# Projecting q and k transposed in the first stage of an AdaLN attention and mixture-of-experts block

## The chip, the cores and the metric

The kernel runs on one core of a Trainium2 chip. A core has five engines with a queue of their own each: TensorE (PE; PEld is its weight load), VectorE (DVE), ScalarE (ACT), GpSimd (POOL) and SyncE (SP), which here only issues DMAs. They work side by side and wait for each other through semaphores. SBUF is the working memory of 128 partitions, PSUM the memory of eight banks (128 x 512 float32 each) that TensorE writes. The metric is the time on the device in microseconds (us); lower is better.

## The reference, cut to what matters

```python
# x: (16, 1024, 256) float32; 16 heads of 16 numbers
mod = (silu(c) @ wmod).reshape(16, 6, 1, -1)      # sa, ca, ga, sb, cb, gb
h = layernorm(x) * (1 + ca) + sa
# attention of h:
xn = (h - mean(h)) * rsqrt(var(h) + 1e-5) * ln_gamma + ln_beta
q, k, v = heads(xn @ Wq + bq), heads(xn @ Wk + bk), heads(xn @ Wv + bv)
# rotation: x1 = even, x2 = odd numbers of a head
rot = stack([x1 * cos - x2 * sin, x1 * sin + x2 * cos], -1)
probs = softmax(causal(rot(q) @ rot(k).T / 4))
x = x + ga * (h + (probs @ v) @ Wo + bo)
h = layernorm(x) * (1 + cb) + sb
x = x + gb * moe_ffn(h)      # 8 experts, 512 chosen rows each, gathered and scattered
```

The change concerns everything from `h` up to the rotated q and k, and the constants that it needs.

## The kernel before, in words

The program is five stages, one after the other, with a barrier of all engines between two of them. `phase0` loads weights and makes the modulation rows and the biases. `phase1` normalises twice, projects q, k and v, rotates q and k and stores them. `phase2` is the attention, `phase3` the output projection and the residual, `phase4` the experts.

`phase1` goes over 16 batches of 1024 rows, eight tiles of 128 rows (T = 8) each. The order on every engine is written out by hand. The function `both(fr, bk)` does the "back" of one batch (`bk`: transpose, project, rotate, store) tile by tile, with pieces of the "front" of the next (`fr`: the two normalisations) put between the tiles. Buffers that hold a batch are double (index `p`), those of a tile too (`t % 2`).

Per tile of the back: PE transposes the normalised rows `xn` (L675), ACT copies them to `x_t` (L552), and PE projects: a bias row by a matmul with three rows of ones (L686) and two matmuls (L688) for q and k together, 128 x 512, then the same for v, 128 x 256. The weights move through the array and the rows of `x_t` are stationary, so rows lie on partitions in the result. DVE multiplies the 512 columns by cosines (L474) and by sines (L475), and adds the two results crosswise with strides (L481, twice 256 columns). PE transposes the rotated tile (L696), and only now do the numbers of a head lie on partitions. The result is kept as three bfloat16 parts: ACT casts the high part (L569), DVE takes the rest (L490), ACT casts the middle part (L575), POOL takes the low part (L641). ACT copies v to `v_st` (L561).

Per batch of the front: DVE takes the statistics of x (L419, L427) and inverts the deviation (L434, L436), ACT makes `h1`, the normalised x (L545), POOL multiplies and adds the modulation (L625, L627) and forms the residual in two more passes (L634, L636). DVE takes the statistics of h (L443, L450), ACT the root (L537), and DVE writes `xn` by eight tensor_scalar instructions in a row after tile 6 (L456, L461). SP loads the batch three ahead, stores the residual (L371), v (L377), and then q and k in 24 DMAs of 64 partitions (L383).

A PSUM bank serves one purpose: 0 and 1 the transposed rows, 2 and 3 q and k of a tile, 4 and 5 v, 6 and 7 the transposed q and k.

Of the kernel before, what the change touches and what calls it, by code (L numbers as in the profile page):

```python
# [25 lines left out]
P = 128  # L26
HEADS = 16
NG = 4
# [32 lines left out]
def build(nc, a, out):  # L61
# [14 lines left out]
    bias_d = nc.dram_tensor("bias_parts", [3, 3 * D], BF16, kind="Internal").ap()  # L76
# [11 lines left out]
    with ExitStack() as outer:  # L88
# [3 lines left out]
        rope = keep("rope", [P, T, 2 * DH], F32)  # L92
        w_all = keep("w_all", [P, KC, 3 * D], F32)
        wo = keep("wo", [P, KC, D], F32)
        bias3 = keep("bias3", [3, 3 * D], BF16)
# [3 lines left out]
        phase0(nc, a, ps, ident, mask, rope, w_all, wo, bias3, ones3, mods_d, bias_d, out_bias_d, b2_d, tok_d)  # L99
        phase1(nc, x, ps, ident, rope, w_all, bias3, ones3, mods_d, resid_d, q_d, k_d, v_d)  # L100
# [6 lines left out]
def phase0(nc, a, ps, ident, mask, rope, w_all, wo, bias3, ones3, mods_d, bias_d, out_bias_d, b2_d, tok_d):  # L107
# [3 lines left out]
    T = rope.shape[1]  # L111
    scale = (D // HEADS) ** -0.5
    with ExitStack() as ctx:
# [10 lines left out]
        brow = sb("brow", [1, 3 * D], F32)  # L124
# [8 lines left out]
        beff = sb("beff", [1, 3 * D], F32)  # L133
        beff_rest = sb("beff_rest", [1, 3 * D], F32)
        beff3 = sb("beff3", [1, 3, 3 * D], BF16)
# [11 lines left out]
        bias_done = sem("p0_bias_done")  # L147
        rows_done = sem("p0_rows_done")
# [11 lines left out]
            (brow[:, 0:D], a["L0_attn_bq"].rearrange("(o n) -> o n", o=1)),  # L160
            (brow[:, D:2 * D], a["L0_attn_bk"].rearrange("(o n) -> o n", o=1)),
            (brow[:, 2 * D:3 * D], a["L0_attn_bv"].rearrange("(o n) -> o n", o=1)),
# [9 lines left out]
        ]  # L172
        LOADED = DMA * (len(loads) + len(small))

        @block.sync
        def _(sp):
            for dst, src in loads:
                sp.dma_start(dst, src).then_inc(loaded, DMA)
            with nc.allow_non_contiguous_dma("one column per contraction chunk"):
# [17 lines left out]
        def _(act):  # L197
            act.wait_ge(loaded, LOADED)
            nc.scalar.activation(e[:, :], c[:, :], ACT.Exp, scale=-1.0).then_inc(exp_done, 1)

        @block.tensor
        def _(pe):
# [12 lines left out]
            for bank, lo, hi in ((4, 0, 2 * D), (5, 2 * D, 3 * D)):  # L215
                for k in range(KC):
                    last = pe.matmul(ps[0:1, bank, 0:hi - lo], beta[:, k:k + 1], w_raw[:, k, lo:hi],
                                     start=(k == 0), stop=(k == KC - 1))
# [1390 lines left out]
```

## Time and profile before

| | |
|---|---|
| median of 3 runs | 3257.47 us (3256.44 to 3257.87) |
| profiled execution | 3256.85 us, its span 3255.1 us |
| busy, whole span | PE 91%, DVE 72%, ACT 53%, POOL 31% |
| mean granted TensorE clock | 0.952 of 2.4 GHz |
| phase0 | 0 to 47 us |
| phase1 | 47 to 763 us |
| phases 2 to 4 | 763 to 3255 us |

The span is what the profiler saw between the first and the last instruction; 1.75 us lie around it. A busy time counts an instruction from its start to its end, whatever it waits for in between; neighbouring instructions of one engine overlap by some tenths of a microsecond, so the distance from one start to the next says what an instruction costs in a queue, and the duration what its result costs to wait for. The granted clock is 1.00 (2.4 GHz) or 0.50 (1.2 GHz) at any instant, and between them only as a mean.

### The profile page before, as it was taken

What the parts mean: (1) busy time and instruction counts of PE and PEld (TensorE: products, weight loads), DVE (VectorE), ACT (ScalarE), POOL (GpSimd) and SP (SyncE); (2) the same over time, 40 slices, a digit from 0 to 9 for tenths busy, and PEclk for the clock granted to TensorE, in tenths of its full rate; (3) what the DMA queues carried; (4) which work ended last, traced back from release to release, by engine and by line L of the source; (5) the groups of instructions that cost most, each with busy time, mean ns of one, the idle gap of its engine ahead of it and who ended that gap; (6) DMA issues with size and microseconds to landing.
All of it is one profiled execution on the core that took longest, in us unless ns stands there. A gap on an engine that the chain in (4) does not pass through costs nothing. (4 is left out here: it accounts for less than half of the span.)

```text
span 3255.1 us, 50330 instructions
## 1 busy us (share of the span) xinstructions
PE 2952.9 (91%) x18199; PEld 1403.3 (43%) x18199; DVE 2328.9 (72%) x3444; ACT 1713.4 (53%) x3591; POOL 1019.2 (31%) x1366
## 2 busy tenths in 40 slices
PE   2888998885999999999999999999999979975997
PEld 0444444441444444444444444444444347753664
DVE  5999999995777777777777777777777425543221
ACT  1444444430677777777777777777777731111111
POOL 3888888862122111112221111112221100003232
PEclk7999999996999999999999999999999989987999
DMA  2466666657244444444444444444444246663332
GB/s 77 138 180 191 191 191 191 184 156 175 55 95 93 95 100 100 100 96 92 94 95 92 97 100 100 100 96 90 95 92 92 48 173 259 259 230 110 78 100 56
DMA packets 175373, 403.11 MB, mean 124 GB/s; under 512 B 34556, under 2 KB 87202, under 8 KB 158518
## 3 DMA queue, kind: packets, MB, share of 16 engines
q1 hardware_dynamic: 168984, 391.37, 47.1%
q0 software_dynamic: 6144, 8.52, 1.5%
q8 instruction: 147, 2.41, 0.3%
q14 instruction: 98, 0.80, 0.1%
HBM read 240.65 MB, written 161.31 MB: 123 GB/s over the span
## 5 line engine op out<-in xcount | busy, mean ns | idle before, releaser
L946 DVE TENSOR_REDUCE mx<-ps 128x2 f32<-128x1024 f32 (+3 forms) x1216 | 1371.2, 1166 | 396.6 <-PE ps L1034 301.3
L992 ACT ACTIVATE prob<-ps 128x512 f32<-128x512 f32 (+1 forms) x2560 | 1251.4, 561 | 539.0 <-PE ps L1052 530.0
L1027 PE MATMUL ps<-k_rows,q_rows 96*128 96x512 bf16 (+3 forms) x3072 | 909.9, 332 | 40.6 <-DMA k_rows<-k_parts 33.1
L1052 PE MATMUL ps<-q_rows,k_rows 99*128 99x512 bf16 (+3 forms) x3072 | 908.5, 329 | 14.5 <-ACT prob L992 6.0
L885 POOL TENSOR_SCALAR_AFFINE_SELECT prob<-prob 128x512 f32<-128x512 f32 x512 | 318.6, 634 | 1453.8 <-ACT prob L992 1453.8
L1071 PE MATMUL ps<-prob,v_rows 128*32 128x512 f32 (+3 forms) x6144 | 628.6, 497 | 0.0
L1052 PEld LDWEIGHTS ps<-q_rows,k_rows 99*128 99x128 bf16 x3072 | 273.3, 98 | 598.8 <-ACT prob L992 359.8
L688 PE MATMUL ps<-w_all,x_t 128*128 128x512 f32 (+1 forms) x1024 | 427.9, 543 | 0.0
L1027 PEld LDWEIGHTS ps<-k_rows,q_rows 96*128 96x128 bf16 x3072 | 290.4, 98 | 269.8 <-DVE mx L946 60.4
L1034 PE MATMUL ps<-mask_b,unit_b 128*128 128x128 bf16 (+2 forms) x1408 | 348.5, 248 | 0.0
L1071 PEld LDWEIGHTS ps<-prob,v_rows 128*32 128x32 f32 x6144 | 134.7, 108 | 245.7 <-ACT prob L992 122.8
L688 PEld LDWEIGHTS ps<-w_all,x_t 128*128 128x128 f32 x1024 | 183.5, 200 | 125.4 <-issue 104.0
L481 DVE TENSOR_TENSOR qr<-m 128x256 f32<-128x256 f32 x256 | 224.2, 958 | 4.4
L641 POOL TENSOR_TENSOR stage<-rest,stage 128x512 bf16<-128x512 f32 x128 | 167.5, 1308 | 119.3 <-ACT stage L575 119.2
L1201 ACT COPY n_t<-ps 128x256 f32<-128x256 f32 x128 | 47.6, 372 | 232.7 <-PE ps L1223 232.7
L1469 DVE SCALAR_TENSOR_TENSOR y<-ps,gx,gate 128x256 f32<-128x256 f32 x32 | 15.5, 484 | 195.7 <-PE ps L1560 192.3
L1034 PEld LDWEIGHTS ps<-mask_b,unit_b 128*128 128x128 bf16 x1408 | 139.2, 99 | 22.8
L1235 PE MATMUL ps<-wg,n_t 128*128 128x256 f32 x512 | 145.7, 407 | 0.0
L561 ACT COPY v_st<-ps 128x256 f32<-128x256 f32 x128 | 47.7, 373 | 178.1 <-PE ps L688 178.1
L675 PE MATMUL ps<-ident,xn 128*128 128x128 f32 x256 | 55.9, 304 | 87.1 <-DVE xn L461 87.1
L1190 DVE TENSOR_TENSOR x<-ps,res_b 128x256 f32<-128x256 f32 x128 | 54.3, 425 | 106.2 <-PE ps L1235 106.2
L1560 PE MATMUL ps<-w,hid 128*128 128x256 f32 x512 | 119.1, 386 | 0.0
(143 smaller groups left out, 2707.4 us busy)
## 6 DMA issues: line engine op xcount, KB each, us to landing
k_rows<-k_parts SPq DMA_DIRECT2D x384, 128.0 KB, 7.5
v_ones<-v_st SPq DMA_DIRECT2D x64, 512.0 KB, 9.0
v_rows<-v_ones SPq DMA_DIRECT2D x64, 512.0 KB, 9.5
att<-o_sb SPq DMA_DIRECT2D x128, 256.0 KB, 3.2
att_b<-att SPq DMA_DIRECT2D x16, 2048.0 KB, 10.9
q_parts<-stage SPq DMA_DIRECT2D x192, 128.0 KB, 2.4
k_parts<-stage SPq DMA_DIRECT2D x192, 128.0 KB, 2.4
q_rows<-q_parts SPq DMA_DIRECT2D x64, 384.0 KB, 4.6
```

Of the source, the lines that this page charges most:

```text
L481: ins = dve.tensor_tensor(dst[:, :, :, :, e], src(m1)[:, :, :, :, e], src(m2)[:, :, :, :, 1 - e], ALU.add)
L641: pool.tensor_tensor(stage[:, p, 2, :, t * P:(t + 1) * P], rest[:, t % 2, :].rearrange("p (a n) -> p a n", a=4), stage[:, p, 1, :, t * P:( ...
L688: ins = pe.matmul(o, x_t[:, t % 2, k, :], w_all[:, k, lo:hi], start=False, stop=(k == KC - 1))
L885: pool.affine_select(out=own, in_=own, compare_op=ALU.is_ge, fill=0.0, base=0, pattern=[[0, HG], [1, P]], channel_multiplier=-1).then_inc( ...
L946: dve.tensor_reduce(dst, src, AX.X, ALU.max).then_inc(a_free, 1)
L992: nc.scalar.activation(prob[:, (g * NPC + i) % RING, h, 0:w], src, ACT.Exp).then_inc(exp_done, 1)
L1027: ins = pe.matmul(ps[:, at, col:col + w], q[0:ROWS, g, h, i * P:(i + 1) * P], k[0:ROWS, g, h, k0:k0 + w], start=(r == 0), stop=True, skip_ ...
L1034: ins = pe.matmul(own, unit_b[:, :], mask_b[:, :].rearrange("p (o n) -> p o n", o=1) .to_broadcast([P, per, P]), start=False, stop=True, s ...
L1052: ins = pe.matmul(ps[:, PS_B + bank(g, n), at:at + w], k[0:AUG, g, h, j * P:(j + 1) * P], q[0:AUG, g, h, q0:q0 + w], start=True, stop=True)
L1071: ins = pe.matmul(ps[32 * h:32 * h + 32, PS_O, col:col + w], v[:, g, j, h, :], prob[:, (g * NPC + i) % RING, h, at:at + w], start=(j == 0) ...
L1235: ins = pe.matmul(o, n_t[:, r % 2, k, :], wg[:, p, k, :], start=False, stop=(k == KC - 1))
L1560: ins = pe.matmul(o, hid[:, f, c * P:(c + 1) * P], w2[:, e % 2, f, :], start=False, stop=(f == FT - 1))
```

## The change

q and k are projected transposed. The weight columns are sorted in `phase0` so that all even numbers of the 16 heads (128 columns) come first, then all odd ones, for q and for k. In `project` the sorted weights are stationary and 512 rows of the input move (L701 of the changed kernel), so that each result fills one bank: the even half of q, the odd half, the same for k. A "pair" is q or k of half a batch, so a batch has four pairs (NP = 4) and `both` has eight half steps j = 0 to 7: even j projects and multiplies a pair, odd j combines it. The bias is a number per partition and goes in with the multiplication by a table of cosines or sines that is itself transposed (L497). The transposes of q and k, their bias matmuls and the strided adds are gone.

The second normalisation moves from DVE (`xn`) to ACT, in place in `h` (L574, `second_norm`), the addition of the modulation from POOL to DVE (L463, `shift_h`), and the residual is formed in place in `h1`. q and k are stored in 16 DMAs of 32 partitions instead of 24 of 64. `phase0` loads the biases of q and k in 16 small DMAs and sorts weights and tables. Phases 2 to 4 are as before.

```diff
@@ phase0
+            cols = a[name].rearrange("(g h i e) -> e g i h", g=NG, h=HG, e=2)
+            for odd in range(2):
+                for g in range(NG):
+                    small.append((braw[32 * g:32 * g + 32, 2 * which + odd:...], cols[odd, g]))
...
+                        ins = dve.tensor_copy(w_raw_p[:, k, 2 * which + odd, :]..., src[:, odd])      # x8
...
+                    ins = dve.tensor_copy(rope_x[:, tab, :, 32 * g:32 * g + 32]..., ...)              # x8
...
@@ phase1, vector
+            def shift_h(b, tiles):
+                for t in tiles:
+                    dve.wait_ge(h_mul, b * T + t + 1)
+                    dve.tensor_tensor(h[:, b % 2, t, :], h[:, b % 2, t, :], mods[:, b % 2, M_SA, :], ALU.add)
...
-                dve.tensor_tensor(view(m1[:, s, :]), view(bank), tab(0), ALU.mult)
-                dve.tensor_tensor(view(m2[:, s, :]), view(bank), tab(1), ALU.mult).then_inc(rope_mul, 1)
+            def multiply(n):
+                for m, table in ((m1, cos_t), (m2, sin_t)):
+                    for e in range(2):
+                        c = 2 * which + e
+                        ins = dve.scalar_tensor_tensor(m[:, e, :], ps[:, PS_QK + c, :], bcol[:, c:c + 1],
+                                                       table[:, at], ALU.add, ALU.mult)
+            def combine(n):
+                dve.tensor_tensor(qr[:, s, 0, :], m1[:, 0, :], m2[:, 1, :], ALU.subtract)
+                dve.tensor_tensor(qr[:, s, 1, :], m1[:, 1, :], m2[:, 0, :], ALU.add).then_inc(rope_done, 1)
+            def take_rest(n):
+                dve.wait_ge(hi_done, n + 1)
+                reuse(dve, lo_done, n - 1)
+                dve.tensor_tensor(rest[:, n % 2], qr[:, n % 2], parts(n, 0), ALU.subtract)
@@ phase1, scalar
+            def second_norm(b, tiles):
+                if 0 in tiles:
+                    act.wait_ge(stath, b + 1)
+                for t in tiles:
+                    nc.scalar.activation(h[:, p, t, :], h[:, p, t, :], ACT.Identity, bias=nmh..., scale=rsh...)
@@ phase1, tensor
+            def project(b, n):
+                pe.wait_ge(xt_copied, b * T + 4 * blk + 4)
+                reuse(pe, rope_mul, n - 1)
...
+                        ins = pe.matmul(ps[:, PS_QK + c, :], w_all[:, k, c * P:(c + 1) * P], x_t[:, blk, k, :], ...)
@@ phase1, sync
-                        for part in range(3):
-                            sp.dma_start(dst[b, g, part], stage[64 * (g % 2):64 * (g % 2) + 64, ...])
+                    for e in range(2):
+                        for g in range(NG):
+                            sp.dma_start(dst[b, g, :, 32 * e:32 * e + 32, :]..., stage[32 * g:32 * g + 32, ...])
```

On ACT, around the end of a batch, before: the root of h, two tiles of the back, then the first tile of the next batch and the root of the x after it.

```order
L537 ACTIVATE sd<-agh,eps 128x8
L552 COPY x_t<-ps 128x256
L561 COPY v_st<-ps 128x4x4x16
L569 CAST stage<-ps 128x4x128
L575 CAST stage<-rest 128x4x128
L561 COPY v_st<-ps 128x4x4x16
L569 CAST stage<-ps 128x4x128
L575 CAST stage<-rest 128x4x128
L552 COPY x_t<-ps 128x256
L537 ACTIVATE sd<-agx,eps 128x8
```

The same place in the changed kernel (half steps 5 to 7).

```order
L558 ACTIVATE sd<-agh,eps 128x8
L591 COPY v_st<-ps 128x4x4x16 x2
L603 CAST stage<-rest 128x2x512
L574 ACTIVATE h<-h,nmh,rsh 128x256 x4
L599 CAST stage<-qr 128x2x512
L582 COPY x_t<-ps 128x2x128 x2
L574 ACTIVATE h<-h,nmh,rsh 128x256 x4
L591 COPY v_st<-ps 128x4x4x16 x2
L603 CAST stage<-rest 128x2x512
L582 COPY x_t<-ps 128x2x128 x2
L558 ACTIVATE sd<-agx,eps 128x8
```

Eight normalisations and two wide casts now stand ahead of the copies of `x_t` on which the next batch's first projection waits. On PE the same place before: the last tile's projection, the transposes of the next batch's first rows, and its projection.

```order
L686 MATMUL ps<-bias3,ones3 128x512
L688 MATMUL ps<-w_all,x_t 128x512 x2
L686 MATMUL ps<-bias3,ones3 128x256
L688 MATMUL ps<-w_all,x_t 128x256 x2
L696 MATMUL ps<-ident,qr 128x128 x4
L675 MATMUL ps<-ident,xn 128x128 x4
L686 MATMUL ps<-bias3,ones3 128x512
```

And in the changed kernel (L690 transposes, L701 is `project`, L708 and L710 are v).

```order
L701 MATMUL ps<-x_t,w_all 128x512 x4
L690 MATMUL ps<-ident,h 128x128 x4
L708 MATMUL ps<-bias3,ones3 128x256
L710 MATMUL ps<-w_all,x_t 128x256 x2
L708 MATMUL ps<-bias3,ones3 128x256
L710 MATMUL ps<-w_all,x_t 128x256 x2
L690 MATMUL ps<-ident,h 128x128 x4
L701 MATMUL ps<-x_t,w_all 128x512 x4
L690 MATMUL ps<-ident,h 128x128 x4
```

The first two transposed tiles stand ahead of v of the batch that ends, and a projection of 512 rows needs four transposed tiles where one was enough. On POOL, in the first half of a batch's back, the changed kernel has (L652 multiplies h, L666 is the low part, L659 and L662 the residual):

```order
L652 TENSOR_TENSOR h<-h1,mods_b 128x256 x2
L666 TENSOR_TENSOR stage<-rest,stage 128x2x512
L652 TENSOR_TENSOR h<-h1,mods_b 128x256 x4
L666 TENSOR_TENSOR stage<-rest,stage 128x2x512
L652 TENSOR_TENSOR h<-h1,mods_b 128x256 x2
L666 TENSOR_TENSOR stage<-rest,stage 128x2x512
L659 TENSOR_TENSOR h1<-h1,mods_b 128x256 x2
```

There is one low part of 1024 columns for every two of 512 before, and it stands directly behind the multiplications for which DVE's `shift_h` waits.

## Rows read from the trace of the kernel before

**Rows 1.** Busy time by stretch, all engines; columns: length, PE, PEld, DVE, ACT, POOL, clock, DMA.
```profile
79.20:709.80 630.60, 557.86 (x1923) 275.22 (x1924) 605.61 (x1227) 270.75 (x627) 516.38 (x604) 0.93 0.59 175
709.80:745.70 35.90, 31.43 (x117) 16.56 (x115) 25.36 (x42) 14.80 (x32) 11.71 (x10) 0.93 0.70 218
745.70:763.20 17.50, 0.00 (x0) 0.00 (x0) 0.00 (x0) 0.00 (x1) 0.01 (x1) 0.50 0.82 200
```

**Rows 2.** DVE by line, 79.2 to 709.8 us; busy us, mean ns, idle before.
```profile
L481 DVE TENSOR_TENSOR qr<-m 128x256 f32<-128x256 f32 x240 | 214.5, 976 | 4.1
L461 DVE TENSOR_SCALAR xn<-h,agh,rsh 128x256 f32<-128x256 f32 x120 | 88.1, 803 | 0.5
L443 DVE BATCH_NORM_STATS2 sth<-h 128x6 f32<-128x256 f32 x120 | 43.8, 405 | 19.4 <-POOL h L627 19.4
```

**Rows 3.** DVE in order of time, ten batches' inversions, first and last; start, length.
```profile
280.77 0.19 DVE L456 RECIPROCAL rsh<-sd 128x8 f32<-128x8 f32 x1
...
660.96 0.18 DVE L456 RECIPROCAL rsh<-sd 128x8 f32<-128x8 f32 x1
```

**Rows 4.** DVE and POOL in order of time, two places of batches with a front.
```profile
299.95 0.73 POOL L625 TENSOR_TENSOR h<-h,mods_b 128x256 f32<-128x256 f32 x1
300.00 2.11 DVE L481 TENSOR_TENSOR qr<-m 128x256 f32<-128x256 f32 x2
...
319.14 2.16 DVE L481 TENSOR_TENSOR qr<-m 128x256 f32<-128x256 f32 x2
...
319.41 1.41 POOL L641 TENSOR_TENSOR stage<-rest,stage 128x512 bf16<-128x512 f32 x1
```

**Rows 5.** DVE in order of time in the last batch, where POOL has little.
```profile
718.34 0.69 DVE L474 TENSOR_TENSOR m<-ps,rope 128x512 f32<-128x512 f32 x1 [1.14 <-PE ps L688]
718.95 0.68 DVE L475 TENSOR_TENSOR m<-ps,rope 128x512 f32<-128x512 f32 x1
719.67 1.10 DVE L481 TENSOR_TENSOR qr<-m 128x256 f32<-128x256 f32 x2
```

**Rows 6.** POOL by line where DVE leaves it alone: 58 to 71, then 715 to 745.
```profile
L625 POOL TENSOR_TENSOR h<-h,mods_b 128x256 f32<-128x256 f32 x8 | 5.8, 722 | 4.9 <-ACT h L545 4.9
...
L641 POOL TENSOR_TENSOR stage<-rest,stage 128x512 bf16<-128x512 f32 x9 | 10.4, 1154 | 22.6 <-ACT stage L575 22.5
```

**Rows 7.** DVE by line in the last stages: forms that the change uses.
```profile
L1469 DVE SCALAR_TENSOR_TENSOR y<-ps,gx,gate 128x256 f32<-128x256 f32 x32 | 15.5, 484 | 195.7 <-PE ps L1560 192.3 <-PE ps L1533 3.4
...
L1428 DVE TENSOR_TENSOR twice<-same,later 128x512 f32<-128x512 f32 x8 | 5.5, 692 | 0.3
...
L1402 DVE TENSOR_TENSOR h<-h,mods 128x256 f32<-128x256 f32 x10 | 3.4, 411 | 0.0
```

**Rows 8.** PE in order of time: full clock first, then a batch's end.
```profile
724.63 1.98 PE L688 MATMUL ps<-w_all,x_t 128*128 128x512 f32 x4
...
324.24 0.58 PE L675 MATMUL ps<-ident,xn 128*128 128x128 f32 x2 [2.24 <-DVE xn L461]
...
326.56 3.78 PE L688 MATMUL ps<-w_all,x_t 128*128 128x512 f32 x4
```

**Rows 9.** A stretch at a batch's end, columns as in rows 1.
```profile
324.40:331.20 6.80, 6.22 (x12) 2.23 (x12) 6.77 (x11) 0.37 (x1) 3.71 (x5) 0.50 0.35 116
```

**Rows 10.** ACT in order of time.
```profile
58.24 4.04 ACT L545 ACTIVATE h<-xin,nmx,rsx 128x256 f32<-128x256 f32 x8 [0.47 <-DVE nmx L436]
...
740.18 0.37 ACT L561 COPY v_st<-ps 128x256 f32<-128x256 f32 x1 [2.40 <-PE ps L688]
...
741.10 0.62 ACT L575 CAST stage<-rest 128x512 bf16<-128x512 f32 x1
```

**Rows 11.** SP and DVE in order of time, the start of the program and of phase1's back.
```profile
4.63 0.24 SPq L178 DMA_DIRECT2D brow<-in_L_attn_bk  x1
...
79.28 0.68 DVE L474 TENSOR_TENSOR m<-ps,rope 128x512 f32<-128x512 f32 x1
```

**Rows 12.** SP in order of time, the last stores of phase1.
```profile
753.24 7.66 SPq L383 DMA_DIRECT2D k_parts<-stage  x12
```

More of the change, by code:

```diff
@@ L178, in _ @@
                 sp.dma_start(dst, src).then_inc(loaded, DMA)
-            with nc.allow_non_contiguous_dma("one column per contraction chunk"):
+            with nc.allow_non_contiguous_dma("one column per contraction chunk or rotation half"):
                 for dst, src in small:
@@ new lines, in _ @@
+            dve.memset(eps[:, :], EPS)
+            for b in range(2):
+                for k in range(2):
+                    take_x(b, range(4 * k, 4 * k + 4))
+                join_x(b)
+                if b == 0:
+                    invert_x(0)
+            for k in range(4):
+                shift_h(0, (2 * k, 2 * k + 1))
+            for k in range(4):
+                take_h(0, (2 * k, 2 * k + 1))
+            join_h(0)
+            invert_h(0)
+            steps(both)
+            take_rest(B * NP - 1)
@@ L645, in front @@
-            def front(fr):
-                for t in range(T):
-                    scaled(fr, t)
-                for t in range(T):
-                    residual(fr, t)
-            def both(fr, bk, first=False, more=True):
-                for t in range(T):
-                    if t >= 2:
-                        low(bk, t - 2)
-                    elif not first:
-                        low(before(bk), T + t - 2)
-                    if fr is not None:
-                        for u in (2 * (t % 4), 2 * (t % 4) + 1):
-                            (scaled if t < 4 else residual)(fr, u)
@@ L661, in tail, with scale_h @@
-            def tail(bk):
-                low(bk, T - 2)
-                low(bk, T - 1)
-            pool.memset(v_st[:, :, :, :, :], 1.0).then_inc(ones_set, 1)
-            run(pool, front, both, tail)
+            def scale_h(b, tiles):
+                p = b % 2
+                if 0 in tiles:
+                    pool.wait_ge(mod_in[p], (b // 2 + 1) * DMA)
+                    reuse(pool, xt_done, b * T - T)
+                for t in tiles:
+                    pool.wait_ge(h1_done, b * T + t + 1)
+                    pool.tensor_tensor(h[:, p, t, :], h1[:, p, t, :], mods[:, p, M_CA1, :], ALU.mult).then_inc(h_mul, 1)
@@ new lines, in both @@
+            def both(nx, fr, bk, j):
+                n = bk * NP + j // 2
+                if fr is not None and j < 4:
+                    scale_h(fr, (2 * j, 2 * j + 1))
+                if j % 2 == 0 and n >= 2:
+                    low(n - 2)
+                if fr is not None and j >= 4:
+                    residual(fr, (2 * j - 8, 2 * j - 7))
+            pool.memset(v_st[:, :, :, :, :], 1.0).then_inc(ones_set, 1)
+            scale_h(0, range(T))
+            residual(0, range(T))
+            steps(both)
@@ L717, in phase2 @@
+            for t in range(4):
+                turn_x(0, t)
+            steps(both)
 def phase2(nc, B, L, ps, ident, mask, q_d, k_d, v_d, max_d, att_d):
```

564 lines of the change are left out of this document (275 added, 289 removed).

## The prediction

> **What bounds the kernel now.** The busy times by stretch come first [rows 1]. The change touches 0 to 763 us only; the stages after it are left as they are, and I take their 2492 us as unchanged. Of the 630.6 us in which a batch's back runs beside the next one's front DVE is busy 605.6, PE 557.9, ACT 270.8, POOL 516.4: DVE is the bound there, PE close behind. In the last batch, which has no front beside it, it is the other way: PE 31.4 of 35.9, DVE 25.4. The period of a full batch follows from two inversions nine batches apart [rows 3]: (660.96 - 280.77) / 9 = 42.24 us.
>
> Second, how much of DVE's busy time is work. The view by lines gives 0.98 us for one strided add L481 and 0.80 for one tensor_scalar L461 of 256 columns [rows 2]. In the last batch the pair of L481 takes 1.10 together, beside POOL's front 2.11 [rows 4, 5]. In rows 4 the first of the pair starts 0.05 after POOL's L625 and is done only after it, so an instruction of DVE that reads two SBUF tensors and one of POOL take turns: 0.5 us of waiting counted as busy in each L481. L474, which reads PSUM and one SBUF tensor, takes 0.69 in rows 5 and 0.68 at 79.28 beside POOL's residual [rows 11]: it does not wait. My own tally of 42.24 by start-to-start distances: 16 of L474 and L475 at 0.60, 16 of L481 at 0.55, 8 of L490 at 0.59, 16 statistics at 0.33, 8 of L461 at 0.26, small ones 1.9, in all 32.2; about 1.3 more is waiting for POOL's h (19.4 / 15 [rows 2]); the other 8.7 is turn-taking, 0.36 for each of 24 instructions. So the removal of DVE work is worth its own time, and the question is what happens to the turns.
>
> **DVE after the change**, per full batch. L474 starts 0.61 before L475 [rows 5]; a per-partition pointer adds 0.06 (484 ns with it and PSUM against 411 without [rows 7], of which a few ns are PSUM's), so 16 multiplications of 512 at 0.66 are 10.6. Two SBUF tensors of 512 last 0.692, of 256 0.411 [rows 7], so 256 columns are 0.28; the starts are closer by 0.08 (ten of 256 take 3.4 us together [rows 7], 0.34 each). That gives 8 of `combine` at 0.61, 4.9; 4 of `take_rest` with 1024 columns at 1.17, 4.7; 8 of `shift_h` at 0.34, 2.7. Statistics 5.3, small ones 1.9. Sum 30.0, against 32.2 before: less than it looks, because the strided adds and the tensor_scalars were short in themselves and long in turns.
>
> **The turns.** POOL before: 32 instructions of 256 at 0.722 and 8 low parts of 512 at 1.154 [rows 6]. After: 24 and four of 1024 columns, each 1.154 + 2 x 0.432 = 2.0. One of 256 keeps DVE out for some 0.58 (from 299.95 to where the first L481, 0.55 long, must have begun), one of 512 for 1.0 (319.41, and the pair beside it at 319.14 takes 2.16 though its first half ran at once [rows 4]), one of 1024 by the same slope 1.86. DVE has 20 instructions that take turns; three (one `take_rest` and two `combine` in j = 7) lie before a wait for PE and cost nothing. For the other 17 I walked through a batch with these durations. In j = 1 ACT normalises two tiles, POOL multiplies them, and the low part follows at once; the first `shift_h` gets in after the second multiplication, the other one waits out the low part: 2.9, and 0.5 for the rest of j = 1. The same in j = 2, 2.4. In j = 3 POOL has run dry, 0. In j = 4 the low part stands ahead of `shift_h`, 1.9. In j = 5 the residual runs, 0.8. Together 8.5. By the mean of before it would be 17 x 0.36 = 6.1. I take 8.0, near the walk, because the low parts hold twice as long; the ends are 3.5 (POOL out of step with DVE) and 11.
>
> **The boundary.** In j = 6 the chain goes through other engines: DVE inverts (0.44 until ACT can start), ACT normalises four tiles (4.04 / 8 = 0.50 each [rows 10], 2.0), casts 1024 columns (0.62 for 512, 0.37 for 256 [rows 10], so 1.1, start to start 0.95), copies two tiles (0.55), normalises four more (2.0), copies v twice, the second after PE's v at the low clock (1.2), casts (0.95), copies two tiles (0.6): 8.7 us. Only then PE may project a pair: 1.98 for two matmuls of 512 [rows 8], 3.8 for four. `multiply` of the next batch starts 12.4 after the inversion. DVE's own work in between (0.3 + 2.64 + 1.32 + 1.17 + 1.22 + 0.54 + 0.3) is 7.5, so it is idle for 4.9. Before, it was idle for nothing there: xn was its own work, and PE needed one tile of it.
>
> PE meanwhile stands still from the end of `project` in j = 6, which it can do two pairs ahead, until the first normalised tile, 8 to 11 us by the walk. Before, 2.24 us without work and another 0.57 [rows 8] were followed by 6.8 us at 0.50 [rows 9], and four matmuls of L688 took 3.78 where they take 1.98 at full clock. I expect the low clock once a batch again. It falls in v and the transposes, which ACT's normalisations cover, and I take the projection at full clock; at the low one it adds 3.8.
>
> Per batch then 30.0 + 8.0 + 4.9 = 42.9. PE's own 27.5 (16 x 0.95 + 8 x 1.2 + 8 x 0.32), ACT's 20 and POOL's 25 lie beside it. From the first multiplication to the last batch: 15 x 42.9 - 1.3 (batch 14 takes no statistics of x in j = 5) = 642.2, against 630.6: **+11.6**.
>
> **Around it.** phase0: 16 small loads more and 2 fewer at 0.24 to 0.64 each [rows 11, 12], +5.5, since everything waits for them; 16 copies of 128 and 256 columns before `silu_t`, +4.7; shorter splits of the bias, -2.2. **+8.0** (bounds +4 and +14). The transposed tables lie beside DVE's chain. Start of phase1: the eight additions of `shift_h` alternate with POOL (0.94 each), eight normalisations and four tiles stand before the first projection of 3.8 to 7.5 us instead of one tile before 2: **+6.5** (+3, +9). Last batch: DVE's first multiplication to the last low part, PE 19.9, then 2.6 + 1.2 + 1.2, casts, rest and low part 5.4, 30.4 against 35.9 [rows 1]: **-5.5** (-8, -2). Tail: 24 stores of 0.64 (7.66 / 12 [rows 12]) follow the last low part in the 17.5 us of rows 1; then only the 8 of k do, 5.1 + 2.5: **-9.9** (-10, -6). These stores come from 32 partitions instead of 64.
> The Trainium skill, SBUF — State Buffer, Door 1: The DMA port swizzle, says that partitions 0 to 31 reach the same eight ports as 0 to 63, so a store of half the partitions is not slower per byte. No run here shows it yet; if the eight last stores were bound by eight ports at the page's 189 GB/s, the tail would be an estimated 3 us longer.
>
> Sum: 11.6 + 8.0 + 6.5 - 5.5 - 9.9 = +10.7. The profiled execution of 3256.85 becomes 3267.5; it is 0.6 below the median, so **3268 us**, 0.3% slower.
>
> **The rivals.** About 0.2% is what a measurement of this kernel can tell from no change, 6.5 us, or 0.43 a batch.
> (a) *POOL's relief reaches DVE.* POOL's work falls from 32 to 25 us a batch, and part of the turns falls into DVE's idle time; the turns cost 5.5. 30.0 + 5.5 + 4.9 = 40.4 a batch, -37.5 against the forecast: 3230. For it: 17 instructions instead of 24. Against it: low parts of twice the length right behind what `shift_h` waits for. Faster below 41.7 a batch. Chance 0.30.
> (b) *The projection at a batch's start is at 1.2 GHz.* PE is idle longer than in rows 8, and the clock comes back too late: + 3.8 a batch, 46.7, 3268 + 57 = 3325. Half of that where it hits every other batch: 3297. Chance 0.12.
> (c) *The multiplication takes turns too.* It reads PSUM, a table and a pointer in SBUF; L474 with PSUM and one table did not. 12 of 16 are not before a wait; at 0.36 each +4.3 a batch, 3268 + 65 = 3333. Chance 0.08.
> The Trainium skill, SBUF — State Buffer, names as the VectorE instructions that contend with GpSimd those in a two-port mode or with two SBUF inputs, and does not say whether a pointer counts; by a reading that counts it, (c) is the case, and rows 5 and 11 show only the form without one.
> (d) *The sum comes out near zero*: a batch at 42.2, 3257. Chance 0.15; mine, 3262 to 3290, 0.35.
>
> **How the numbers follow.** The likeliest is 3268, its own range 3258 to 3290. With 0.30 around 3230 and 0.2 above 3290, 80% needs 3228 to 3308. Turns at 3.5 and 11 alone give 3200 and 3313; I leave out the outer part of both. Faster: (a) and a little of the spread, 0.33; within 0.2%: 0.17; slower: 0.50.
>
> **What would show it.** In the profile after: inversions 42.9 us apart; `multiply` (L497) 0.72 to 0.75 long, and the same beside POOL and without it; `shift_h` and `combine` pairs with 0.5 to 1.9 more than alone; DVE idle 4 to 5 us per batch before `multiply`, released by PE L701, and there only; PE idle 8 us or more before the first transpose L690 of a batch, with the granted clock at 0.50 behind it; the first multiplication at 79.3 + 14.5 = 93.8 us; 7 to 8 us from the last low part to phase2. The forecast is wrong if the period is under 41.7, and its reason is wrong if DVE's idle time at the boundary is under 2 us, or if the turns cost under 5 a batch.

## The result and the profile after

The changed kernel takes 3241.87 us (median of 5 runs, 3240.84 to 3243.01), the kernel before beside it 3257.41. The ratio is 0.9953, with a 95% interval of 0.9938 to 0.9968: faster by 0.5%, a small difference but clear of the noise. The forecast was 3268, slower by 0.3%. The time by stretch, with the cuts of [rows 1], in the profiled execution:

| stretch | forecast | measured |
|---|---|---|
| phase0 (to 47.0 before, 58.8 after) | +8.0 | +11.8 |
| start of phase1, to the first multiplication | +6.5 | +4.8 |
| first multiplication to the last batch's | +11.6 | **-19.1** |
| last batch, to its last low part | -5.5 | -5.6 |
| tail, to phase2 | -9.9 | -7.1 |
| the stages behind | 0 | -0.8 |
| sum | +10.7 | -16.0 |

One term is wrong in sign, and it alone is 30.7 us off; the other errors, +3.8 and +2.8 against -1.7, -0.1 and -0.8, hide 4.0 of it. The stretches after (us; busy time of PE, PEld, DVE, ACT, POOL; granted clock):
```profile
95.90:707.30 611.40, 426.05 (x1322) 225.84 (x1321) 556.22 (x1061) 315.35 (x627) 446.42 (x419) 0.84 0.55 179
707.30:737.60 30.30, 21.33 (x72) 11.28 (x70) 22.29 (x29) 14.24 (x22) 10.60 (x5) 0.90 0.79 249
737.60:748.00 10.40, 0.00 (x0) 0.00 (x0) 0.00 (x0) 0.00 (x0) 0.02 (x1) 0.50 0.88 243
```
Inversions nine batches apart, as in [rows 3], give the period, (653.77 - 285.14) / 9 = 40.96 us, against 42.24 before and 42.9 forecast:
```profile
285.14 0.18 DVE L483 RECIPROCAL rsh<-sd 128x8 f32<-128x8 f32 x1
...
653.77 0.18 DVE L483 RECIPROCAL rsh<-sd 128x8 f32<-128x8 f32 x1
```
DVE by line, 95 to 700 us, answering to [rows 2]: the multiplication lasts 0.74 on average, `shift_h` 0.97 where the same form alone lasts 0.41 [rows 7], and one line waits for PE.
```profile
L463 DVE TENSOR_TENSOR h<-h,mods_b 128x256 f32<-128x256 f32 x120 | 111.9, 971 | 0.0
L497 DVE SCALAR_TENSOR_TENSOR m<-ps,bcol,cos_t 128x512 f32<-128x512 f32 x120 | 84.0, 740 | 52.4 <-PE ps L701 52.4
```
The boundary and steps j = 1 and 2 of one batch on DVE (start, length, engine; merged rows such as x2 are instructions back to back), inversion at 448.97:
```profile
458.40 0.17 DVE L457 SCALAR_TENSOR_TENSOR nmx<-agx,rsx 128x8 f32<-128x8 f32 x1
461.56 1.41 DVE L497 SCALAR_TENSOR_TENSOR m<-ps,bcol,cos_t 128x512 f32<-128x512 f32 x2 [3.00 <-PE ps L701]
462.89 1.40 DVE L497 SCALAR_TENSOR_TENSOR m<-ps,bcol,sin_t 128x512 f32<-128x512 f32 x2
464.21 2.85 DVE L463 TENSOR_TENSOR h<-h,mods_b 128x256 f32<-128x256 f32 x2
466.98 1.74 DVE L512 TENSOR_TENSOR rest<-qr,stage 128x1024 f32<-128x1024 f32 x1
...
471.05 1.27 DVE L463 TENSOR_TENSOR h<-h,mods_b 128x256 f32<-128x256 f32 x2
472.24 1.40 DVE L497 SCALAR_TENSOR_TENSOR m<-ps,bcol,cos_t 128x512 f32<-128x512 f32 x2
```
and POOL beside it:
```profile
463.09 1.42 POOL L652 TENSOR_TENSOR h<-h,mods_b 128x256 f32<-128x256 f32 x2 [6.46 <-ACT h L566]
464.47 2.31 POOL L666 TENSOR_TENSOR stage<-rest,stage 128x1024 bf16<-128x1024 f32 x1
...
470.39 1.65 POOL L652 TENSOR_TENSOR h<-h,mods_b 128x256 f32<-128x256 f32 x2 [1.07 <-ACT h L566]
472.00 2.31 POOL L666 TENSOR_TENSOR stage<-rest,stage 128x1024 bf16<-128x1024 f32 x1
```
In j = 1 the second `shift_h` waits out the low part (2.85 for two), as the forecast walked it. In j = 2 it got in before the low part began at 472.00, and behind it stands the multiplication, 1.40 a pair as at 461.56: it reads one SBUF tensor and takes no turn. The low part of 2.3 us there costs DVE next to nothing. In j = 4 a low part stands ahead of `shift_h` again, as forecast:
```profile
479.23 2.64 DVE L463 TENSOR_TENSOR h<-h,mods_b 128x256 f32<-128x256 f32 x2
```

PE at that boundary (after 8 matmuls of L701 that end at 439.4):
```profile
450.42 1.18 PE L690 MATMUL ps<-ident,h 128*128 128x128 f32 x4 [11.05 <-ACT h L574]
...
451.85 2.07 PE L710 MATMUL ps<-w_all,x_t 128*128 128x256 f32 x4
...
457.82 3.70 PE L701 MATMUL ps<-x_t,w_all 128*128 128x512 f32 x8 [1.52 <-ACT x_t L582]
```
v runs at the granted clock of 0.50 (446:454), where four matmul records of 256 columns take 2.07 and not the 1.13 of full clock. From 455.4 on the granted clock is 1.00 again, and the projection, which starts 8.85 after the inversion, takes 3.70, all of it at 2.4 GHz.

### The profile page after: what moved, and what is told of

The parts are those of the page before. It is cut to its first block and busy times, and to the rows that moved or that the text cites. A ratio compares the mean times of both kernels' runs of the same rounds, so it can differ in the third digit from the quotient of the medians.

```text
span 3239.1 us, 48169 instructions
## 1 busy us (share of the span) xinstructions
PE 2817.5 (87%) x17587; PEld 1353.4 (42%) x17587; DVE 2278.7 (70%) x3286; ACT 1765.1 (54%) x3595; POOL 948.2 (29%) x1174
## 5 line engine op out<-in xcount | busy, mean ns | idle before, releaser
L1068 PE MATMUL ps<-q_rows,k_rows 99*128 99x512 bf16 (+3 forms) x3072 | 907.2, 328 | 14.7 <-ACT prob L1008 6.1
L701 PE MATMUL ps<-x_t,w_all 128*128 128x512 f32 x512 | 233.2, 598 | 23.2 <-ACT x_t L582 23.2
L690 PE MATMUL ps<-ident,h 128*128 128x128 f32 x256 | 48.2, 319 | 206.5 <-ACT h L574 203.9
L666 POOL TENSOR_TENSOR stage<-rest,stage 128x1024 bf16<-128x1024 f32 x64 | 147.8, 2309 | 75.5 <-ACT stage L603 75.5
L710 PE MATMUL ps<-w_all,x_t 128*128 128x256 f32 x512 | 167.5, 456 | 0.0
L652 POOL TENSOR_TENSOR h<-h,mods_b 128x256 f32<-128x256 f32 x128 | 111.2, 890 | 121.2 <-ACT h L566 121.1
L701 PEld LDWEIGHTS ps<-x_t,w_all 128*128 128x128 f32 x512 | 95.2, 191 | 121.5 <-issue 92.7
L497 DVE SCALAR_TENSOR_TENSOR m<-ps,bcol,cos_t 128x512 f32<-128x512 f32 x128 | 89.6, 740 | 61.1 <-PE ps L701 61.1
L690 PEld LDWEIGHTS ps<-ident,h 128*128 128x128 f32 x256 | 33.6, 158 | 234.7 <-ACT h L574 223.0
```

Source lines behind the costliest of these rows:

```text
L652: pool.tensor_tensor(h[:, p, t, :], h1[:, p, t, :], mods[:, p, M_CA1, :], ALU.mult).then_inc(h_mul, 1)
L666: pool.tensor_tensor(parts(n, 2), rest[:, n % 2], parts(n, 1), ALU.subtract).then_inc(lo_done, 1)
L701: ins = pe.matmul(ps[:, PS_QK + c, :], w_all[:, k, c * P:(c + 1) * P], x_t[:, blk, k, :], start=(k == 0), stop=(k == KC - 1))
L710: ins = pe.matmul(o, x_t[:, t // 4, k, t % 4 * P:t % 4 * P + P], w_all[:, k, 2 * D:3 * D], start=False, stop=(k == KC - 1))
L1068: ins = pe.matmul(ps[:, PS_B + bank(g, n), at:at + w], k[0:AUG, g, h, j * P:(j + 1) * P], q[0:AUG, g, h, q0:q0 + w], start=True, stop=True)
```

## The experiments

All times are medians, with the range; the changed kernel (3241.9) is the base, and "before" ran beside each (3257.1 to 3257.7). What is said of single batches is read from the one profiled execution of each.

**1. A small instruction ahead of j = 2's `shift_h`** on DVE.
```diff
+                if fr is not None and j in (2,):
+                    dve.memset(spare_t[:, 0:240], 0.0)
```


> The changed kernel with one idle memset of 240 columns (about 0.25 us of DVE, no SBUF input, so it takes no turn with POOL) ahead of the shift_h of half step 2 in 15 batches. Theory T (the turn between shift_h and POOL's low part in j=2 decides; the forecast lost it by 0.2 us): now the second shift_h waits out the low part, the period goes from 40.96 to about 42.9 and the kernel to about 3270. Rival R1 (only own time counts): +0.25 a batch, 3246. Rival R2 (DVE has slack): 3242, no change.


3256.82 (3255.73 to 3258.24), +1.0 us a batch for 0.18 to 0.26 us of work; nobody had that. The placement in j = 2 held (two `shift_h` 1.22, multiplication at once behind them). The extra came elsewhere: batches of 41.3, 41.6 and 43.4 us in turn, and in the five long ones the first multiplication came 14.7 to 14.9 after the inversion, not 12.7 to 13.0. There the projection took 5.4 to 5.6 where the others have 3.70, at a mean granted clock of 0.65 to 0.68. These five are some 10 of the 15 us: a second cause, at the boundary.

**2. ACT's last four second normalisations behind the copies of tiles 2 and 3.**


> The changed kernel with the second half of the second normalisation (ACT, tiles 4 to 7) moved behind the copies of x_t on which the next batch's first projection waits. Theory T (the ACT chain j=6 to j=7 sets when the projection starts, and DVE idles 3.4 us for it): chain 2.0 us shorter, DVE's idle time down by 2.0, period 39.0, kernel about 3212. Rival R1 (PE's v at the low clock or the turns of DVE in j=7 take its place): period 40.5 to 41, kernel 3235 to 3242. Rival R2 (turns in j=1, 2 and 4 grow again because DVE meets POOL elsewhere): slower than 3242.


3242.88 (3240.38 to 3243.73), no change. ACT now waits for v where it worked before, and the first multiplication stays where it was:
```profile
457.82 0.37 ACT L591 COPY v_st<-ps 128x256 f32<-128x256 f32 x1 [1.58 <-PE ps L712]
```
The rival was right: v at half clock takes ACT's place in the chain.

**3. The 16 small bias loads on a semaphore of their own**, waited for only where `bcol` is added up.
```diff
-                    sp.dma_start(dst, src).then_inc(loaded, DMA)
+                    sp.dma_start(dst, src).then_inc(loaded if i < 2 else late, DMA)
...
+            dve.wait_ge(late, DMA * LATE)
             link(dve.tensor_tensor(bcol[:, :], ps[:, 4, 0:512:128], braw[:, :], ALU.add))
```


> The changed kernel with the 16 small loads of the q and k biases on a semaphore of their own, for which only the addition of the biases in phase0 waits. Theory T (they hold up the whole start, 22.8 against 12.7 us): -9 to -10 us, about 3232. Rival (the small descriptors delay the large loads on the queues themselves): -2 us or less.


3232.65 (3232.27 to 3233.15), -9.2, as the theory had it. In the changed kernel ACT's first instruction waited 20.72 us, for the last of them:
```profile
22.81 0.42 ACT L216 ACTIVATE e<-c 16x256 f32<-16x256 f32 x1 [20.72 <-DMA braw<-in_L_attn_bk]
```
With the loads apart it starts at 13.05, where the kernel before has 12.69.

**4. POOL's low part in j = 0 ahead of its multiplications of h**, so that it is not right behind them.
```diff
+                if j == 0 and n >= 2:
+                    low(n - 2)
                 if fr is not None and j < 4:
                     scale_h(fr, (2 * j, 2 * j + 1))
-                if j % 2 == 0 and n >= 2:
+                if j in (2, 4, 6) and n >= 2:
                     low(n - 2)
```


> The changed kernel with POOL's low part of half step 0 ahead of the multiplications instead of behind them; its input is ready about 6 us before POOL starts there. Theory T (the second shift_h of j=1 waits 1.9 us for this low part): that wait goes, period 39.1 and kernel about 3214. Rival R1 (what follows in j=1 and j=2 meets POOL's multiplications instead): half of it, about 3228. Rival R2 (no gain, the time reappears before the multiplication, where PE is late): 3242.


3226.88 (3224.40 to 3242.34), -15, ratio to before 0.9917 (0.9888 to 0.9945). The four executions differ: two at 3224, the profiled one at 3229, and one at 3242, no faster than the changed kernel. The profiled run has two kinds of batch, seven of 38.5 to 39.4 us and then 40.95. In both the two `shift_h` of j = 1 take 0.92 together, where the changed kernel has 2.85. They differ in PE's projection at the boundary; below are such a pair of `shift_h`, and a projection of each kind:
```profile
656.54 0.92 DVE L463 TENSOR_TENSOR h<-h,mods_b 128x256 f32<-128x256 f32 x2
...
285.51 3.70 PE L703 MATMUL ps<-x_t,w_all 128*128 128x512 f32 x8 [1.52 <-ACT x_t L582]
...
648.61 5.25 PE L703 MATMUL ps<-x_t,w_all 128*128 128x512 f32 x8 [1.10 <-ACT x_t L582]
```
The granted clock is 1.00 over 285:289 and 0.50 over 641:649, so the second one began at half clock. So a turn of 1.9 is worth 1.5 to 2.4 a batch, and the clock can take all of it back (40.95 is the changed kernel's period). The median is the first rival's 3228, but the batches of the first kind are the theory's 39.1; what is missing to its 3214 lies in the others. The mean granted clock of the whole execution is 0.936 in the two at 3224, 0.933 in the one at 3229 and 0.928 in the one at 3242.

**5. The turn of j = 2 put back**: the low part between the two multiplications of h, where the forecast had DVE meet it.
```diff
-                    scale_h(fr, (2 * j, 2 * j + 1))
+                    scale_h(fr, (2 * j,))
...
                     low(n - 2)
+                if fr is not None and j == 2:
+                    scale_h(fr, (2 * j + 1,))
```


> POOL's low part in step j = 2 goes between the two multiplications of h instead of behind both. Theory T: the forecast's walk had the low part of j = 2 hold up the second shift_h for 1.9 us, in the changed kernel it runs beside the multiplication, and that one place is most of what the forecast was wrong by. Put ahead of the second shift_h it holds DVE up: +1.9 us a batch, 15 batches, 3242 + 28 = 3270; the second shift_h of j = 2 about 2.8 instead of 0.95. Rival R1: DVE's later work takes the wait up (fewer turns in j = 3 and 4), under +0.5 a batch, 3242 to 3249. Rival R2: the batch leaves the step it keeps with the granted clock (13.65 us of half clock per 40.96), and the projection falls into the low clock in some batches: +2.1 more in every third batch, about 3280.


3284.26 (3265.47 to 3286.06, 9 runs), ratio 1.0055 (1.0034 to 1.0075). The number is a mixture: four runs lie at 3265.5 to 3266.1 (mean granted clock 0.932 to 0.933), five at 3284.3 to 3286.1 (0.923 to 0.924). The lower ones are +24, 1.6 us a batch. The profiled run is of the upper kind, 44.36 a batch:
```profile
478.46 0.63 DVE L449 BATCH_NORM_AGGREGATE agx<-stx 128x2 f32<-128x6 f32 x8
...
484.96 1.41 DVE L497 SCALAR_TENSOR_TENSOR m<-ps,bcol,cos_t 128x512 f32<-128x512 f32 x2 [4.80 <-PE ps L705]
...
494.45 2.68 DVE L463 TENSOR_TENSOR h<-h,mods_b 128x256 f32<-128x256 f32 x2
497.05 1.40 DVE L497 SCALAR_TENSOR_TENSOR m<-ps,bcol,cos_t 128x512 f32<-128x512 f32 x2
```
The two `shift_h` of j = 2 take 2.68 and not 1.27, +1.4; and DVE waits 4.80 for PE and not 3.00: the projection began at half clock and took 5.35 instead of 3.70. With ACT's root 0.2 later that is +2.0, the clock's part. The second rival had foreseen it, for every third batch; here it is in every one from the fourth on. No execution of the lower kind was profiled, but three early batches of this one have the turn and a projection at full clock. They take 43.07, 41.87 and 42.73, on average 1.6 more than 40.96, which is what the lower kind shows. The third of them:
```profile
215.02 3.70 PE L705 MATMUL ps<-x_t,w_all 128*128 128x512 f32 x8 [1.35 <-ACT x_t L582]
...
228.26 2.67 DVE L463 TENSOR_TENSOR h<-h,mods_b 128x256 f32<-128x256 f32 x2
```
The forecast's walk had the price of the turn nearly right and its place wrong.

**6. PE kept at work through its pause**: 20 matmuls whose result nobody reads.
```diff
+                if fr is not None and j == 6:
+                    fill(bk, 20)
                 if fr is not None and j >= 6:
                     for t in (2 * j - 12, 2 * j - 11):
                         turn_x(fr, t)
```


> 20 matmuls of 128x512 whose result nobody reads, on PE in step j = 6 between the last projection of a batch and the first transpose of the next (PE has no work there for 11.05 us; 20 x 0.45 = 9.0). They change no output. Theory T: the granted clock falls to 0.50 because PE stands still, so with the filler it stays at 1.00, the transposes and v behind it take half, copy_v no longer waits, and ACT alone sets the boundary: the projection 0.5 to 1 us earlier, 3242 - 8 to -15 = 3227 to 3234. Rival R1: the clock falls anyway, for a reason that lies in the work and not in the pause; the filler then takes up to 18 us at half clock, and the transposes wait for it: +7 a batch, 3345. Rival R2: the clock stays up, but what ACT does sets the time: 3240 to 3243.


3298.10 (3297.55 to 3299.92). The size was wrong: a matmul of 512 columns in fp32 is two records of 0.43, so the filler took 17.33 us and held the transposes up. On the clock the theory was right: 1.00 over the whole loop, against 0.83 in the changed kernel over the same stretch.
```profile
95.00:700.00 605.00, 585.22 (x1740) 294.01 (x1739) 508.67 (x979) 283.68 (x568) 404.09 (x381) 1.00 0.55 168
```
So the work itself doesn't lower the clock here. Which pause does, the runs don't settle: 1.52 before the projection is left here, and the clock stayed, while in experiment 13 it fell behind one of 1.44.

**7. The same with 9.**


> The filler again, in the right size: a matmul of 128x512 in fp32 is two records of 0.43, so the 20 of the experiment before took 17.3 us and held the transposes up; 9 take 7.8 of the 11.05 us in which PE stands still. Theory T: the granted clock stays at 1.00 through the boundary, v is done by 4.7 after the inversion, ACT's chain ends at 8.4 instead of 8.9, and every batch has the projection at full clock: -0.3 to -0.6 a batch, 3233 to 3238. Rival R1: the 3 us of pause that are left are enough for the clock to fall, no change, 3242. Rival R2: the later ACT work was not the limit and the projection comes 2 us earlier, 3212.


3239.94 (3239.16 to 3240.57), 1.9 below the changed kernel, which is less than can be told apart (6.5, by the forecast). Periods are 40.5 and 41.3 in turn and the clock's mean 0.94, but with 3.3 us of pause left it still fell before or during v, four records of which take 2.08. The first rival was right.

**8. The turn of j = 2 and the filler of 9 together.**


> The low part of j = 2 between the two multiplications of h (which alone gave 44.36 a batch, 3284) together with the filler of 9 matmuls (which alone gave 40.5 to 41.4 a batch, 3240). Theory T: of the 3.4 us a batch, 1.4 is the turn of DVE with the low part and 2.0 the projection at half clock behind it; with the filler only the turn is left: 41.0 + 1.4 = 42.4 a batch, 3240 + 21 = 3261. Rival R1: both parts belong to the order of the low part, and the filler changes nothing: 3280 to 3290. Rival R2: without the half clock the batch is short enough for the turn to fall elsewhere: 3240 to 3250.


3287.44 (3262.31 to 3288.91, 10 runs), again two kinds: three at 3262 to 3266, seven at 3287 to 3289. In the profiled run PE paused for 4.72 us behind the filler, then v and the beginning of the projection were at half clock:
```profile
461.70 7.89 PE L712 MATMUL ps<-x_t,w_all 128*128 128x512 f32 x18
474.31 1.18 PE L694 MATMUL ps<-ident,h 128*128 128x128 f32 x4 [4.72 <-ACT h L574]
...
482.10 5.34 PE L705 MATMUL ps<-x_t,w_all 128*128 128x512 f32 x8 [1.10 <-ACT x_t L582]
```
So the filler does not keep the upper kind away. What separates the kinds is the projection and the clock: 5.34 and 5.35 against 3.70, and a mean granted clock of 0.937 to 0.938 in all seven upper executions against 0.952 to 0.953 in the three lower ones. One batch of the profiled run has the turn (2.67) and a projection of 3.70, and it takes 42.25, the theory's 42.4. Why one execution of a program falls into one kind and the next into the other stays open.

**9. v of tiles 6 and 7 ahead of the transposes**, with experiment 2's move.


> v of tiles 6 and 7 is put ahead of the next batch's first transposes on PE (PE stood still there for 11.05 us), and ACT's last four second normalisations go behind the copies of tiles 2 and 3, as in the experiment before that moved those alone and gave nothing. Theory T: that one gave nothing because copy_v then waited for v at half clock; with v done ahead, ACT's chain from the inversion to the projection is 0.7 + 2.1 + 1.0 + 0.5 + 0.5 + 1.0 + 0.6 = 6.4 instead of 8.9, DVE's idle time at the boundary falls from 3.4 to about 1, 15 x -2.3 = -34: 3208. Rival R1: the projection moves forward into the stretch at half clock and takes 5.3 instead of 3.7 for its pair: 15 x -0.7, 3231. Rival R2: another wait ends there, no change, 3242.


3253.41 (3252.29 to 3254.97), +11.5: neither number. The projection came forward by only 1.2 us, to 7.6 after the inversion, since ACT's cast of `rest` waits for DVE (L512) there, and now it began at half clock:
```profile
545.82 5.39 PE L703 MATMUL ps<-x_t,w_all 128*128 128x512 f32 x8 [2.32 <-ACT x_t L582]
```
That is the first rival's mechanism, and dearer than it said: over the batches of the profiled run the projection takes 5.10 to 6.75, on average 5.8. So 2.1 is lost for 1.2 won, 0.9 a batch or 13 in all, near the measured 11.5.

**10. The second normalisation back on DVE.**


> The second normalisation goes back to DVE, four tiles in j = 6 and four in j = 7; nothing else. Theory T: DVE is the bound, it gets 8 x 0.26 more of its own and takes turns with POOL's residual, 8 x 0.80 by the mean of before is an upper end; the projection of the next batch comes after DVE's j = 7 instead of after ACT, so the idle time at the boundary does not shrink by as much: +3 to +5 a batch, 3242 + 45 to 75 = 3287 to 3317. Rival R1: the 3.4 us in which DVE is idle at the boundary take the work up: within 0.5 a batch, 3235 to 3250, and the move of the normalisation to ACT was worth nothing.


3292.18 (3290.48 to 3292.56), +50, within the theory's range; 43.9 us a batch, and in four of them 45.5 to 45.9, where the projection begins at half clock. In j = 6 and 7 DVE gets 2.59 and 1.37 of normalisations, and still waits for the projection, 3.15 in most batches and 4.86 in this one of the long kind:
```profile
478.17 2.59 DVE L490 TENSOR_SCALAR h<-h,agh,rsh 128x256 f32<-128x256 f32 x4
...
484.33 1.37 DVE L490 TENSOR_SCALAR h<-h,agh,rsh 128x256 f32<-128x256 f32 x4
...
492.10 1.41 DVE L502 SCALAR_TENSOR_TENSOR m<-ps,bcol,cos_t 128x512 f32<-128x512 f32 x2 [4.86 <-PE ps L706]
```
So placed, four in j = 6 and four in j = 7, the rest of the change without this move is 35 us slower than the kernel before; another placement was not tried.

**11. The shift of h back on POOL.**


> The shift of h goes back to POOL, as it was before the change: 8 additions of 256 columns, DVE only waits for them ahead of its statistics. Theory T: DVE is the bound, it loses 2.7 us of its own and the 5 us that these eight wait for POOL, and gets turns on rest and combine and waits for h in exchange (before had 1.3 of waiting and 0.36 a turn on 24 instructions): 2 to 4 us a batch less, 3182 to 3212. Rival R1: POOL (25 + 5.5 of work, with its turns 36 or more of 41) becomes the chain: multiplication, shift and low part in a row hold the statistics of h up, so the move to DVE was needed: 3242 to 3270.


3244.13 (3239.65 to 3245.11): no difference that can be told. DVE loses `shift_h`, 111.9 us over the loop, and gets most of that back as a wait of the statistics and longer turns; L507 is 1211 ns where it was 805:
```profile
L507 DVE TENSOR_TENSOR qr<-m 128x512 f32<-128x512 f32 x59 | 71.4, 1211 | 0.0
L471 DVE BATCH_NORM_STATS2 sth<-h 128x6 f32<-128x256 f32 x120 | 44.9, 415 | 56.9 <-POOL h L650 56.9
```
Theory T is refuted. The time lies at the lower end of the rival's 3242 to 3270, and its wait for POOL is there, but its conclusion isn't: the move of the shift was worth nothing either way.

**12 to 14. Towards a faster version.** The edits of experiments 3 and 4 with a filler of 9 matmuls:


> Three edits together: the 16 small bias loads on a semaphore of their own (-9.2 alone), POOL's low part of j = 0 ahead of its multiplications (-15 alone, where 7 batches took 39.2 and the later 8 took 40.95 with the projection at half clock), and the filler of 9. Theory T: that experiment's second kind of batch was the granted clock's doing, the filler makes all 15 like the first kind and 0.45 shorter: 3226.9 - 9.2 - 12 - 7 = 3199. Rival R1: the two kinds come from the order of POOL's and DVE's instructions, not from the clock: 3210 to 3218.


3213.07 (3212.63 to 3217.43), in the rival's range but not by its reason: the batches of 38.6 have a projection of 3.70, those of 40.3 and 41.0 one of 5.4 to 5.6, so the kinds go with the clock as the theory had it, and the filler did not keep it up.

Experiments 2, 3, 4 and 9 together, with `high` of j = 6 ahead of the normalisations and `middle` of j = 7 behind the copies, so that no cast stands between ACT's copies and the projection, and 6 matmuls of filler (shown against experiment 2):
```diff
+                if j == 6:
+                    high(n - 1)
                 if fr is not None and j == 6:
                     second_norm(fr, range(4))
...
+                if j == 7:
+                    middle(n - 1)
                 if nx is not None and j == 7:
                     root(nx, 0, agx, agx_done, sdx_done)
                 if fr is not None and j == 7:
                     second_norm(fr, range(4, T))
```


> Everything that shortens the boundary together: loads apart, low part first in j = 0, the last four second normalisations behind the copies of tiles 2 and 3, high of j = 6 ahead of the first four and middle of j = 7 behind those copies, v of tiles 6 and 7 ahead of the transposes, and 6 matmuls of filler ahead of v. Theory T: the projection can start some 5.3 after the inversion instead of 8.9, the first multiplication at 9.6 instead of 12.6, so the boundary's 3.4 us of idle DVE go: 39.3 - 3.0 = 36.3 a batch, 3242 - 9 - 70 = 3163, up to 3190 if the later normalisations make new turns. Rival R1: ACT's middle part and first normalisation come later and hold POOL and DVE up by as much: 3200 or more.


3186.30 (3182.54 to 3190.97), ratio 0.9783 (0.9767 to 0.9800): 23 us short of the theory's best, inside its range. The clock fell here although PE's longest pause at the boundary is 1.44 in the batches of 37.54.

The same without the filler:


> The fastest version so far (3186.3, 37.54 a batch) without its 6 filler matmuls. Theory T: the half clock comes back into the projection and its v, up to 2 us a batch where it does: 3195 to 3216. Rival R1: the reordering alone gives all of it, 3183 to 3190, and the filler can be left out.


**3183.65** (3182.77 to 3185.92), ratio to before 0.9775 (0.9759 to 0.9792), 2.25% faster than before. The rival was right, the filler can go. Its boundary on PE and DVE, in batches of 37.54 us:
```profile
495.77 6.24 PE L712 MATMUL ps<-x_t,w_all 128*128 128x512 f32 x8 [0.46 <-ACT x_t L585]
...
500.37 0.79 DVE L460 SCALAR_TENSOR_TENSOR nmx<-agx,rsx 128x8 f32<-128x8 f32 x1
502.04 1.41 DVE L500 SCALAR_TENSOR_TENSOR m<-ps,bcol,cos_t 128x512 f32<-128x512 f32 x2 [0.88 <-PE ps L712]
```
The multiplication comes 11.1 after the inversion, not 12.6, though the projection still begins at half clock: its eight matmul records take 6.24 and not 3.70.

## Why the prediction was wrong, point by point

**The step that failed** is "The turns": "Together 8.5 ... I take 8.0, near the walk". By start-to-start distances less the own times (one instruction of DVE starts 0.08 before the one ahead of it ends, not some tenths), in the batch shown:

| step | forecast | measured | from |
|---|---|---|---|
| j = 1 | 3.4 | 3.1 | 2.77 - 0.68 for two `shift_h`, 0.5 + 0.5 for rest and combine |
| j = 2 | 2.4 | 0.5 | 1.19 - 0.68 |
| j = 3 | 0 | 0 | 0.69 - 0.68 |
| j = 4 | 1.9 | 1.9 | 2.56 - 0.68 |
| j = 5 | 0.8 | 0.5 | |
| sum | 8.5 (taken 8.0) | 6.0 | |

Of the walk's 2.5 too many, j = 2 is 1.9, and 15 x (8.0 - 6.0) = 30 us is nearly the term's whole error of 30.7. "The same in j = 2" assumed that the low part follows the multiplications before DVE has its second `shift_h`; but DVE's second `shift_h` stood waiting from about 471.4 and the low part came at 472.00, 0.6 too late; the pair takes 1.27 in all 14 batches after the first. The low part then lay beside an instruction that takes no turn. Experiment 5 shows it: put in the assumed place, the low part costs 1.6 us a batch, +24, and gives a kernel at 3265.5, near the forecast of 3268. Experiment 4 shows the same price at another place: it takes out the turn of j = 1 and gains 1.5 to 2.4 in the batches with the projection at full clock. The mean of before, 17 x 0.36 = 6.1, had stood in the text as the other estimate. Its number came out, but partly by luck: 4.0 of the 6.0 are two waits for a low part, in j = 1 and j = 4, and not 17 turns of 0.36. The Trainium skill, SBUF — State Buffer, SBUF: two separate sides, says that of a VectorE instruction with two SBUF inputs and a GpSimd one that reads SBUF the first to start gets the shared port pair for the whole instruction. The trace agrees (2.68 against 1.27 for the same two instructions), and it is why 0.6 us in who comes first decides over 1.4 to 1.9. It is also why the 0.18 of experiment 1 didn't move the place.

**Own time** was right: 40.96 - 6.0 - 5.1 (next point) = 29.9, forecast 30.0 (its items add up to 30.1, and those of the tally before to 32.4, not 32.2; neither changes anything). Multiplications start 0.66 apart, as forecast. They last 0.74 beside POOL and alone (0.741 to 0.751 in the last batch), so rival (c) is refuted.

**The boundary** was right: the first multiplication at 12.60 against 12.4, so 5.1 of time that is not DVE's own work against 4.9. Of these 3.43 show as idle and the rest as turns in j = 7. PE's pause is 11.05 ("8 to 11"). The balance with [rows 2, 3]: own time -2.2, turns 8.7 to 6.0, waits 1.3 to 5.1; together -1.1 for the measured -1.28. By the forecast's own signs its reason was not refuted, since the turns cost over 5 and DVE's idle time is over 2; only the period, under 41.7, says that it is wrong.

**The clock** was right for this kernel, by luck of its place: v at 0.50, and the projection at full clock, which was back 2.4 before it, so rival (b) didn't happen here. It is no remote case: of the experiments only 6 and 7 are free of it behind the first batch, and 1, 4, 5 and 8 to 14 each had it in several batches or in all. Its price was not the 3.8 of the forecast, since only the beginning of the projection is slow: 5.2 to 5.6 instead of 3.70 in most, 6.24 in experiment 14 and up to 6.75 in experiment 9.

**Rival (a)** came nearest in number: POOL's relief, turns 5.5, 40.4 a batch, 3230 against 40.96 and 3241.9. Its mechanism isn't shown. The turn that the walk had and the run had not is that of j = 2, and there it is the order that saves it, not POOL's lighter load; no run changes the load alone.

**phase0** was mis-sized, within its bounds: +11.8 for +8.0. The loads cost 9.2 (experiment 3) to 10 (22.81 - 12.69) and not 5.5: the issue of one takes 0.72 us and not the 0.24 to 0.64 of [rows 11, 12]:
```profile
9.92 5.83 SPq L198 DMA_DIRECT2D braw<-in_L_attn_bq  x8
15.80 5.63 SPq L198 DMA_DIRECT2D braw<-in_L_attn_bk  x8
```
**Start of phase1** +4.8 for +6.5 and **last batch** -5.6 for -5.5 are within their bounds. **Tail**: -7.1 for -9.9. The stores of q are issued only from 733.35, behind the low part that ends at 733.26, and hold the queue until k's follow:
```profile
733.35 6.13 SPq L417 DMA_DIRECT2D q_parts<-stage  x8
739.59 5.60 SPq L417 DMA_DIRECT2D k_parts<-stage  x8
```
The forecast had q's eight issued before the last low part (end 737.62); the last of them were behind it, and k's first comes 2.0 later. Then the issue of k's eight, 5.6, and 2.8 more make the 10.4. For 32 partitions, which reach eight ports, the Trainium skill, SBUF — State Buffer, Door 1: The DMA port swizzle, gives 189 GB/s at 1 MiB. The stores together moved 243 GB/s in this stretch (737.60:748.00 above), so that limit did not bound them together, and the 3 us are not seen.

**What the change is made of**, by the experiments: the second normalisation on ScalarE instead of VectorE, placed as in experiment 10, is worth 50 us (some 7 of them the clock's), the rest of the change costs 35, the shift's place nothing.

## What to carry to other kernels

Where two engines take turns at a shared resource, a walk through the order is only as good as its closest race: find the pairs that are decided by less than the walk's own error, price both outcomes, and weigh the walk against the mean turn measured before. Put a long instruction of the one engine where the other runs something that takes no turn; one line of order was worth 15 us here, and another cost 24. A chain through a pause of PE has two lengths, one for each granted clock, and shortening it can move its matmuls into the slow stretch.

## What the runs showed of the hardware that was not expected

- A DMA of 32 elements into 32 partitions holds the issuing queue for 0.72 us (11.46 us for 16), against 0.40 to 0.49 for most of the large contiguous ones, and everything that waits for the last of them starts 10 us later.
- The same program has executions 19 and 25 us apart (3265.5 and 3285 in experiment 5, 3262 to 3266 and 3288 in experiment 8), and the mean granted clock tells them apart without exception (0.933 and 0.923, 0.952 and 0.937). In the upper one's trace the projection begins at the granted clock of 0.50. It is a kind that repeats from batch to batch once it is there: periods of 40.96, 44.36 and 37.54 hold to 0.03 us, the last from the seventh batch on.
- With PE busy through the boundary the clock was 1.00 for 605 us; with pauses of 3 to 5 us left it fell in nearly every batch, and in experiment 13 with none longer than 1.44 there.
